# A graph propagation kernel: VectorE's running sums and first-segment sums of a batch in two runs instead of in pairs

## The chip, the core and the metric

The kernel runs on one core of a Trainium2 chip. The metric is the device time of one execution in microseconds (us). The core has a matrix engine (TensorE, PE in the rows), VectorE (DVE), ScalarE (ACT), GpSimd (POOL) and SyncE (SP), which run side by side and meet at semaphores. In this kernel SyncE starts the plain loads and stores, and GpSimd starts the indirect ones, the gathers, which fetch one table row for each of 128 partitions by an index in SBUF.

## What is computed

Four graph layers on 50000 nodes of 96 channels and 50000 edges sorted by destination, each added to its input behind a layer norm and a relu. The change touches the third, a personalised-PageRank propagation:

```python
def _L2_gnn_ref(x, edge_index):
    K = 16
    ALPHA = 0.1
    ...
    norm = (deg_inv_sqrt[row] * deg_inv_sqrt[col])[:, None]
    h = x
    for _ in range(K):
        h_neighbors = jax.ops.segment_sum(norm * h[row], col, num_segments=N)
        h = (1.0 - ALPHA) * h_neighbors + ALPHA * x
    return h
```

So 16 times over, each edge fetches the row of its source, and the rows of one destination are summed.

## The kernel before

The edges lie in order of destination, 392 per partition (`CH`), and are worked in `NB` = 49 batches of `J` = 8 columns, so a batch is 8 gathers of 128 rows of 96 floats. The sums over a destination's edges are made as a scan along each partition: `S[j] = S[j-1] * keep[j] + g[j]`, where `keep` is 0 where a new destination begins. Beside it runs `F = F + g[j] * first[j]`, the sum of the edges that belong to the first destination of the partition. It is needed only when the round is over, where a product with the matrix `B` carries sums across partitions.

The first round (`r1`) has a program of its own. The other 15 (`ROUNDS` - 1) are one hardware loop, `rounds`, with all five engines in one block, and `skewed` lets each engine take its steps on batch b with a fixed lag:

- GpSimd: `gathers`, 8 indirect DMAs from the table `y_t` of the round before into `g_` (names `r_g` in rows, line L340). There are `GB` = 4 buffers. Before a batch it waits for its indices (`s_ix`) and for VectorE to have ended batch b - 4 (`s_ss`).
- VectorE: `scan_step` (L349 running sums into `S`, rows `r_S`; L351 first-segment sums into `F`), 16 SCALAR_TENSOR_TENSOR of 128x96 floats with three inputs each, two tensors and one column of scalars. `own.settle()` behind each pair waits until both have ended. The last op of the batch increments `s_ss` ("r_sums").
- TensorE: `add` (L1421) adds `S` to the PSUM banks `pu` by products with the identity, as soon as `s_ss` has counted the batch; `start` (L1415, L1416) has put the other terms there for the next batch.
- ScalarE: `value` (L1443) scales the eight columns out of PSUM into `H`; `slots` (L1435, L1437) copies indices and scan factors for a later batch.
- SyncE: `store` (L1381) writes the batch's `H` into the other `y_t`, then `load` (L1376) fetches the constant term of a later batch.

A round begins on GpSimd only when all stores of the round before have landed (`s_st`) and so has the row of first values (`s_zo`, stored at L1386), since it gathers from that table. Between the rounds VectorE runs `finish_round` (L1248 to L1251), which waits for the product `r_pc` (L1427) and reads `F`.

Semaphores keep the name that they first got in this program. In the rows of the instruction order below `n0_ones` is VectorE's own count (`s_v`), `info_vector` is `s_ss`, `e0_ea_in_0` is the new `s_ff`, `gathered2_2` counts landed gathers, `n0_vector_stats` is `s_ix` and `n0_vector_scale` is `s_up`.

Of the kernel before, what the change touches and what calls it, by code (L numbers as in the profile page):

```python
# [19 lines left out]
D = 96  # L20
# [4 lines left out]
J = 8  # L25
NB = CH // J
# [4 lines left out]
GB = K  # L31
# [17 lines left out]
ALU = mybir.AluOpType  # L49
# [108 lines left out]
def program(nc, x, src, dst, edge_attr_32, edge_attr_96, edge_weight,  # L158
# [26 lines left out]
    with outer:  # L185
# [158 lines left out]
        def scan_step(dve, own, h, w, g, S, slots=2, s_s=None, done=None):  # L344


            for j in range(J):
                before = S[:, (h - 1) % slots, J - 1, 0:w] if j == 0 else S[:, h % slots, j - 1, 0:w]
                own.add(V.scalar_tensor_tensor(out=S[:, h % slots, j, 0:w], in0=before, scalar=scan_s[:, h, j, 0:1],  # L349
                                               in1=g[:, j, 0:w], op0=ALU.mult, op1=ALU.add))  # L350
                last = V.scalar_tensor_tensor(out=F[:, 0:w], in0=g[:, j, 0:w], scalar=scan_s[:, h, j, 1:2],  # L351
                                              in1=F[:, 0:w], op0=ALU.mult, op1=ALU.add)
                if j < J - 1 or s_s is None:
                    own.add(last)
                else:
                    last.then_inc(s_s, 1)
                own.settle()
            if s_s is not None:
                dve.wait_ge(s_s, done)

        def pointers(own, ptr, no, start, t, to, base):

# [867 lines left out]
        with ExitStack() as p5:  # L1230
# [29 lines left out]
            with nc.Block() as block:  # L1260
# [52 lines left out]
                def _(dve):  # L1313
# [16 lines left out]
                    def step(n, h):  # L1330
# [24 lines left out]
            s_v, s_ix, s_g, s_up, s_s, s_st, s_ss = (sem("r_vector"), sem("r_rows_set"), s_stream[2],  # L1355
                                                     sem("r_summed"), sem("r_values"), sem("r_stored"), sem("r_sums"))
            s_c = sems("r_start_loaded")
            s_cr, s_z, s_zo = sem("r_carry"), sem("r_first_values"), sem("r_first_stored")

            def rounds(eng, one):  # L1360
# [6 lines left out]
            with nc.Block() as block:  # L1367
# [23 lines left out]
                @block.gpsimd  # L1391
                def _(pool):
                    def one(r, odd):

                        after(pool, s_st, 16 * NB * r)
                        after(pool, s_zo, 16 * r)
                        pool.sem_inc(s_turn_p)

                        def step(b, n, h):
                            after(pool, s_ix, 2 * (r * NB + b) + 2)  # L1400
                            after(pool, s_ss, r * NB + b + 1 - GB)
                            gathers(y_t[odd], lambda j: g_[:, h % GB, j, :], h, s_g[h])
                        skewed(pool, (0, step))
                    rounds(pool, one)
# [25 lines left out]
                @block.scalar  # L1430
                def _(act):
                    def one(r, odd):
                        def slots(b, n, h):
                            s_g.wait(act, h, 16 * J * (r * OF[h] + n))
                            A.copy(idx_s[:, h, :], cols(yptr_e, b)).then_inc(s_ix, 1)  # L1435
                            after(act, s_ss, r * NB + b - 3)
                            A.copy(scan_s[:, h], cols(scan, b)).then_inc(s_ix, 1)  # L1437

                        def value(b, n, h):
                            after(act, s_up, r * NB + b + 1)  # L1440
                            v, k = cols(H, b), cols(k_e, b)
                            for j in range(J):
                                last = A.activation(v[:, j, :], pu[h % 2][j // 4][:, j % 4, :], ACT.Copy,  # L1443
                                                    scale=k[:, j:j + 1])
                            last.then_inc(s_s, 1)
                        after(act, s_ss, r * NB)
                        skewed(act, (-2, slots), (1, value))
                    rounds(act, one)

                @block.vector  # L1450
                def _(dve):
                    own = Own(dve, s_v)
                    per_batch = 2 * J - 1
                    per_round = NB * per_batch + 3

                    def one(r, odd):
                        def step(b, n, h):
                            own.base, own.n = r * per_round + b * per_batch, 0
                            after(dve, s_ix, 2 * (r * NB + b) + 2)
                            after(dve, s_up, r * NB + b - 1)  # L1460
                            s_g.wait(dve, h, 16 * J * (r * OF[h] + n + 1))
                            scan_step(dve, own, h, D, g_[:, h % GB], S, 2, s_ss, r * NB + b + 1)
                            assert own.n == per_batch
                            dve.sem_inc(s_turn_v)
                        skewed(dve, (0, step))
                        own.base, own.n = r * per_round + NB * per_batch, 0
                        finish_round(dve, own, s_cr, r + 1, zs, s_z)
                        assert own.n == 3
                        dve.wait_ge(s_z, r + 1)
                        dve.sem_inc(s_turn_v)  # L1470
                    rounds(dve, one)
# [272 lines left out]
```

## Time and profile before

| | us |
|---|---|
| median of 3 runs | 15979.43 |
| lowest and highest | 15961.53, 15987.55 |
| span of the profiled execution | 13552.9 |
| lying outside the span, against the median | 2426.5 |

The profiled execution has no device time of its own on the page; the span runs from its first to its last instruction. The propagation loop is the stretch from 4275 to 11926 us of it, 7.65 ms. In the rows a line of the timeline has the start in us, the duration in us, then engine, line, operation and tiles, and in brackets how long the engine sat idle before it and what released it. "issue" is time in which the engine waited for nothing that the profile shows. Several instructions can stand merged in one row (x2, x8).

### The profile page before, as it was taken

Reading aid. Unit: us, or ns where it says so; the run is one execution under the profiler, and the core shown is the slowest. Engines: PE = TensorE matmul, PEld = TensorE weight load, DVE = VectorE, ACT = ScalarE, POOL = GpSimd, SP = SyncE. Lnnn points to the kernel's source line nnn. Section 1 sums busy time; section 2 is a strip of 40 time slices with the busy share of each in tenths; the row PEclk is TensorE's granted clock in tenths of the full one; section 3 lists DMA queues with packets and bytes.
Section 4 is the critical chain, followed back from the end, with each engine's and each line's share of the span. In section 5 each row is a group of like instructions: output and inputs, shape, how many; then the busy total and the mean of one; then the engine's idle time right before and its main releaser. Section 6 shows DMA issues by size and latency. Waiting matters only on the chain. (4 is left out here: it accounts for less than half of the span.)

```text
span 13552.9 us, 124135 instructions
## 1 busy us (share of the span) xinstructions
PE 6161.5 (45%) x16702; PEld 3564.8 (26%) x16702; DVE 6176.6 (46%) x21955; ACT 3099.7 (23%) x11470; POOL 9980.6 (74%) x10210
## 2 busy tenths in 40 slices
PE   6422105873002555555555555555555555544000
PEld 4322103542001322223323332323322322233000
DVE  4344455596343444444444444444444444444533
ACT  5300133394000222222222222222222222233000
POOL 7677777676777777777777777777777777777777
PEclk8655557886555777777777777777777777755555
DMA  5433353374223333333333333333333333344245
GB/s 150 120 99 100 109 145 97 92 216 142 76 75 89 117 112 112 118 112 112 116 112 112 118 112 112 116 112 112 117 112 112 116 113 112 116 132 129 73 116 140
DMA packets 855833, 1558.86 MB, mean 115 GB/s; under 512 B 321698, under 2 KB 378674, under 8 KB 855666
## 3 DMA queue, kind: packets, MB, share of 16 engines
q1 hardware_dynamic: 523217, 1053.28, 22.9%
q0 software_dynamic: 332448, 504.04, 16.3%
q14 instruction: 148, 1.20, 0.0%
q8 instruction: 20, 0.33, 0.0%
HBM read 954.90 MB, written 602.08 MB: 115 GB/s over the span
## 5 line engine op out<-in xcount | busy, mean ns | idle before, releaser
L340 POOL DMA_INDIRECT r_g<-y_t,idx_s x6272 | 6051.0, 965 | 2128.7 <-issue 2115.0
L349 DVE SCALAR_TENSOR_TENSOR r_S<-r_S,scan_s,r_g 128x96 f32<-128x96 f32 x6272 | 2020.3, 322 | 4670.1 <-DMA r_g<-y_t,idx_s 3968.8
L1421 PE MATMUL r_pu<-r_S,ident 128*128 128x384 f32 x2940 | 1883.7, 787 | 3127.9 <-DVE F L351 3127.9
L1443 ACT ACTIVATE H<-r_pu,k_e 128x96 f32 (+1 forms) x5880 | 1443.3, 356 | 6059.3 <-PE r_pu L1421 6059.3
L351 DVE SCALAR_TENSOR_TENSOR F<-r_g,scan_s,F 128x96 f32<-128x96 f32 x6272 | 1967.6, 314 | 0.0
L1421 PEld LDWEIGHTS r_pu<-r_S,ident 128*128 128x128 f32 x2940 | 737.9, 276 | 3947.0 <-DVE F L351 3583.5
L1415 PE MATMUL r_pu<-H,ident 128*128 (+1 forms) x2940 | 1633.0, 646 | 101.5 <-DMA r_c<-c_t 101.5
L340 POOL DMA_INDIRECT n_ag<-agg_t,idx_s x1176 | 1227.2, 1044 | 395.8 <-issue 368.4
L1416 PE MATMUL r_pu<-r_c,ident 128*128 128x384 f32 x2940 | 1441.4, 578 | 0.0
L1415 PEld LDWEIGHTS r_pu<-H,ident 128*128 128x128 f32 x2940 | 824.4, 281 | 816.9 <-issue 683.4
L1416 PEld LDWEIGHTS r_pu<-r_c,ident 128*128 128x128 f32 x2940 | 712.4, 242 | 599.2 <-issue 383.0
L340 POOL DMA_INDIRECT e_g<-z_t,idx_s x392 | 397.2, 1013 | 148.5 <-issue 120.8
L340 POOL DMA_INDIRECT n_y<-y_t,idx_s x392 | 403.0, 1028 | 135.4 <-issue 118.0
L751 PE MATMUL e_eo<-w_e,e_eaT 97*128 97x96 f32 x784 | 182.7, 428 | 676.3 <-ACT e_eaT L772 676.3
L1297 PE MATMUL r_pc<-r_S,B 128*128 128x96 f32 x2 | 0.7, 475 | 1059.9 <-DVE H L1342 1059.9
L556 POOL DMA_INDIRECT info_t<-seg_s,idx_s x392 | 382.1, 975 | 120.2 <-issue 119.2
L1289 POOL DMA_INDIRECT r_c<-y_t,r_dst_s x392 | 378.0, 964 | 119.5 <-issue 119.5
L340 POOL DMA_INDIRECT e_kv<-kv_t,idx_s x392 | 377.9, 964 | 119.4 <-issue 119.4
L340 POOL DMA_INDIRECT e_x<-rec_t,idx_s x392 | 375.4, 958 | 119.4 <-issue 117.0
L731 POOL DMA_INDIRECT e_q<-q_t,dst_s x392 | 371.2, 947 | 119.5 <-issue 114.3
L349 DVE SCALAR_TENSOR_TENSOR e_S<-e_S,scan_s,e_g 128x96 f32<-128x96 f32 (+1 forms) x1176 | 380.3, 323 | 58.0 <-DVE e_g L800 9.4
L351 DVE SCALAR_TENSOR_TENSOR F<-e_g,scan_s,F 128x96 f32<-128x96 f32 (+1 forms) x1176 | 375.6, 319 | 0.0
(233 smaller groups left out, 7251.4 us busy)
## 6 DMA issues: line engine op xcount, KB each, us to landing
y_t<-H SPq DMA_DIRECT2D x784, 384.0 KB, 2.4
r_c<-c_t SPq DMA_DIRECT2D x735, 384.0 KB
r_g<-y_t,idx_s POOLq DMA_INDIRECT x6272
n_x<-x_t SPq DMA_DIRECT2D x147, 384.0 KB, 4.5
kv_t<-n_kvq SPq DMA_DIRECT2D x49, 768.0 KB, 3.7
agg_t<-e_S SPq DMA_DIRECT2D x98, 384.0 KB, 2.6
x_t<-n_x SPq DMA_DIRECT2D x98, 384.0 KB, 2.4
y_t<-n_y SPq DMA_DIRECT2D x98, 384.0 KB
```

Source lines behind the costliest of these rows:

```text
L340: G.indirect_dma_start(out=to(j), out_offset=None, in_=table, in_offset=bass.IndirectOffsetOnAxis(ap=idx_s[:, h, j:j + 1], axis=0)).then_i ...
L349: own.add(V.scalar_tensor_tensor(out=S[:, h % slots, j, 0:w], in0=before, scalar=scan_s[:, h, j, 0:1], in1=g[:, j, 0:w], op0=ALU.mult, op1 ...
L351: last = V.scalar_tensor_tensor(out=F[:, 0:w], in0=g[:, j, 0:w], scalar=scan_s[:, h, j, 1:2], in1=F[:, 0:w], op0=ALU.mult, op1=ALU.add)
L556: G.indirect_dma_start(out=info_t, out_offset=bass.IndirectOffsetOnAxis(ap=idx_s[:, h, j:j + 1], axis=0), in_=seg_s[:, h, j, :], in_offset ...
L731: G.indirect_dma_start(out=gq[:, h, j, :], out_offset=None, in_=q_t, in_offset=bass.IndirectOffsetOnAxis(ap=dst_s[:, h, j:j + 1], axis=0)) ...
L751: last = T.matmul(eo[g][:, j, :], eaT[:, h, g, j * P:(j + 1) * P], w_e[:], start=True, stop=True)
L1289: G.indirect_dma_start(out=cs[:, h, j, :], out_offset=None, in_=y_t[0][0:ROWS, :], in_offset=bass.IndirectOffsetOnAxis(ap=dst_s[:, h, j:j ...
L1297: T.matmul(pc[:], B[:], S[:, 0, J - 1, :], start=True, stop=True).then_inc(s_cr, 1)
L1415: T.matmul(pu[h % 2][g][:], ident[:], cols(H, b)[:, c, :], start=True, stop=False)
L1416: T.matmul(pu[h % 2][g][:], ident[:], cs[:, h % 2, c, :], start=False, stop=False)
L1421: last = T.matmul(pu[h % 2][g][:], ident[:], S[:, h % 2, 4 * g:4 * g + 4, :], start=False, stop=True)
L1443: last = A.activation(v[:, j, :], pu[h % 2][j // 4][:, j % 4, :], ACT.Copy, scale=k[:, j:j + 1])
```

## The change

In the 15 rounds of the loop VectorE no longer alternates. It does the batch's eight running sums first, each waiting for the one before, then its eight first-segment sums, each waiting for the one before. The eighth running sum increments `s_ss`, the eighth first-segment sum a new semaphore `s_ff`. TensorE still waits for `s_ss`. GpSimd and ScalarE, which need the whole batch to be done before they overwrite `g_` or `scan_s`, wait for `s_ff` instead. `r1` and the other three layers keep `scan_step`.

```diff
+        def running_sums(own, h, g, S, s_s):
+            for j in range(J):
+                before = S[:, (h - 1) % 2, J - 1, 0:D] if j == 0 else S[:, h % 2, j - 1, 0:D]
+                last = V.scalar_tensor_tensor(out=S[:, h % 2, j, 0:D], in0=before, scalar=scan_s[:, h, j, 0:1],
+                                              in1=g[:, j, 0:D], op0=ALU.mult, op1=ALU.add)
+                if j < J - 1:
+                    own.do(last)
+            last.then_inc(s_s, 1)
+
+        def first_sums(own, h, g, s_f):
+            for j in range(J):
+                last = V.scalar_tensor_tensor(out=F[:, 0:D], in0=g[:, j, 0:D], scalar=scan_s[:, h, j, 1:2],
+                                              in1=F[:, 0:D], op0=ALU.mult, op1=ALU.add)
+                if j < J - 1:
+                    own.do(last)
+            last.then_inc(s_f, 1)
...
+            s_ff = sem("r_first_sums")
...
-                            after(pool, s_ss, r * NB + b + 1 - GB)
+                            after(pool, s_ff, r * NB + b + 1 - GB)
...
-                            after(act, s_ss, r * NB + b - 3)
+                            after(act, s_ff, r * NB + b - 3)
...
-                        after(act, s_ss, r * NB)
+                        after(act, s_ff, r * NB)
...
-                    per_batch = 2 * J - 1
+                    per_batch = 2 * J - 2
...
-                            scan_step(dve, own, h, D, g_[:, h % GB], S, 2, s_ss, r * NB + b + 1)
+                            running_sums(own, h, g_[:, h % GB], S, s_ss)
+                            first_sums(own, h, g_[:, h % GB], s_ff)
+                            after(dve, s_ss, r * NB + b + 1)
+                            dve.sem_inc(s_turn_v)
+                            after(dve, s_ff, r * NB + b + 1)
```

VectorE before, in the loop of the rounds, where one batch ends and the next begins:

```order
L349 SCALAR_TENSOR_TENSOR r_S<-r_S,scan_s,r_g 128x96 [waits n0_ones]
L351 SCALAR_TENSOR_TENSOR F<-r_g,scan_s,F 128x96
L75 REGISTER_ALU
L359 REGISTER_ALU [waits n0_ones]
L108 ISA [waits info_vector]
L349 SCALAR_TENSOR_TENSOR r_S<-r_S,scan_s,r_g 128x96 [waits gathered2_2,n0_vector_scale,n0_vector_stats]
L351 SCALAR_TENSOR_TENSOR F<-r_g,scan_s,F 128x96
L75 ISA
```

A first-segment sum stands behind each running sum without a wait, and the next running sum waits for both.

VectorE now, in the middle of a batch, where the last running sums meet the first of the first-segment sums:

```order
L365 SCALAR_TENSOR_TENSOR r_S<-r_S,scan_s,r_g 128x96 [waits n0_ones]
L75 REGISTER_ALU
L365 SCALAR_TENSOR_TENSOR r_S<-r_S,scan_s,r_g 128x96 [waits n0_ones]
L374 SCALAR_TENSOR_TENSOR F<-r_g,scan_s,F 128x96
L75 REGISTER_ALU
L374 SCALAR_TENSOR_TENSOR F<-r_g,scan_s,F 128x96 [waits n0_ones]
```

Every sum now waits for the one before it on its own engine, but for the first of the eight first-segment sums, which follows the last running sum without a wait.

VectorE now, at the end of a batch:

```order
L374 SCALAR_TENSOR_TENSOR F<-r_g,scan_s,F 128x96 [waits n0_ones]
L108 REGISTER_ALU
L108 ISA [waits info_vector,e0_ea_in_0]
L365 SCALAR_TENSOR_TENSOR r_S<-r_S,scan_s,r_g 128x96 [waits gathered2_2,n0_vector_scale,n0_vector_stats]
L75 ISA
```

The running sums stand in front of the first-segment sums that they alternated with, and the batch ends with waits for both semaphores.

## Rows read from the trace of the kernel before

**Rows 1.** The page: busy time by engine, and its costliest group.

```profile
PE 6161.5 (45%) x16702; PEld 3564.8 (26%) x16702; DVE 6176.6 (46%) x21955; ACT 3099.7 (23%) x11470; POOL 9980.6 (74%) x10210
...
L340 POOL DMA_INDIRECT r_g<-y_t,idx_s x6272 | 6051.0, 965 | 2128.7 <-issue 2115.0
```

**Rows 2.** Tile r_g on POOL, loop of the rounds: duration ns min/median/max.

```profile
L340 POOL DMA_INDIRECT r_g<-y_t,idx_s x5876: 941/947/1049, 4275.1 to 11910.6; - x196
```

**Rows 3.** The same instructions, busy us (count) in that stretch.

```profile
4275.00:11911.00 7636.00, 5640.06 (x5876) 0.78 0.38 114
```

**Rows 4.** Tile r_g, a round's first batch, when VectorE is idle.

```profile
L340 POOL DMA_INDIRECT r_g<-y_t,idx_s x8: 943/946/947, 4778.8 to 4787.5; - x8
```

**Rows 5.** Timeline of one batch in the middle of a round.

```profile
6000.54 0.94 POOL L340 DMA_INDIRECT r_g<-y_t,idx_s  x1 [0.30 <-issue]
...
6003.07 0.32 DVE L349 SCALAR_TENSOR_TENSOR r_S<-r_S,scan_s,r_g 128x96 f32<-128x96 f32 x1 [5.40 <-DMA r_g<-y_t,idx_s]
6003.30 0.31 DVE L351 SCALAR_TENSOR_TENSOR F<-r_g,scan_s,F 128x96 f32<-128x96 f32 x1
6003.65 0.32 DVE L349 SCALAR_TENSOR_TENSOR r_S<-r_S,scan_s,r_g 128x96 f32<-128x96 f32 x1
...
6004.23 0.35 DVE L349 SCALAR_TENSOR_TENSOR r_S<-r_S,scan_s,r_g 128x96 f32<-128x96 f32 x1
6004.29 0.95 POOL L340 DMA_INDIRECT r_g<-y_t,idx_s  x1 [0.30 <-issue]
...
6005.43 0.32 DVE L349 SCALAR_TENSOR_TENSOR r_S<-r_S,scan_s,r_g 128x96 f32<-128x96 f32 x1
6005.54 1.02 POOL L340 DMA_INDIRECT r_g<-y_t,idx_s  x1 [0.30 <-issue]
...
6007.43 0.31 DVE L351 SCALAR_TENSOR_TENSOR F<-r_g,scan_s,F 128x96 f32<-128x96 f32 x1
6007.79 0.50 PEld L1421 LDWEIGHTS r_pu<-r_S,ident 128*128 128x128 f32 x2 [5.01 <-DVE F L351]
...
6013.11 0.35 SPq L1381 DMA_DIRECT2D y_t<-H  x1
```

**Rows 6.** Timeline: gathers that start at other distances from a sum.

```profile
8384.49 0.31 DVE L351 SCALAR_TENSOR_TENSOR F<-r_g,scan_s,F 128x96 f32<-128x96 f32 x1
8384.67 0.96 POOL L340 DMA_INDIRECT r_g<-y_t,idx_s  x1 [0.30 <-issue]
...
11539.68 0.31 DVE L351 SCALAR_TENSOR_TENSOR F<-r_g,scan_s,F 128x96 f32<-128x96 f32 x1
11539.82 1.00 POOL L340 DMA_INDIRECT r_g<-y_t,idx_s  x1 [0.30 <-issue]
```

**Rows 7.** Timeline of the end of a round and the start of the next.

```profile
5783.03 0.95 POOL L340 DMA_INDIRECT r_g<-y_t,idx_s  x1 [0.30 <-issue]
...
5785.41 0.32 DVE L349 SCALAR_TENSOR_TENSOR r_S<-r_S,scan_s,r_g 128x96 f32<-128x96 f32 x1 [5.26 <-DMA r_g<-y_t,idx_s]
...
5789.73 0.31 DVE L351 SCALAR_TENSOR_TENSOR F<-r_g,scan_s,F 128x96 f32<-128x96 f32 x1
5790.10 0.50 PEld L1421 LDWEIGHTS r_pu<-r_S,ident 128*128 128x128 f32 x2 [3.60 <-DVE F L351]
...
5793.06 1.96 ACT L1443 ACTIVATE H<-r_pu,k_e 128x96 f32<-128x96 f32 x8 [7.93 <-PE r_pu L1421]
5793.43 0.26 DVE L1248 TENSOR_TENSOR Z<-F,r_pc 128x96 f32<-128x96 f32 x1 [3.39 <-PE r_pc L1427]
...
5795.58 0.36 SPq L1386 DMA_DIRECT2D y_t<-r_zs  x1
...
5799.47 0.94 POOL L340 DMA_INDIRECT r_g<-y_t,idx_s  x1 [15.50 <-issue]
```

**Rows 8.** Timeline of the last stage: a load on SyncE's queue.

```profile
13396.24 0.38 SPq L1671 DMA_DIRECT2D n_z<-z_t  x1
```

**Rows 9.** Chain that ended last, same place: start us, us, what.

```profile
13399.38 3.31 DMA n_ag<-agg_t,idx_s
```

## The prediction, made before the changed kernel ran

> **What bounds the kernel now.** I read the page first, then the tile of the gathers, then the timeline of one batch and of one change of rounds. The page has GpSimd busy for 74% of the span, and its costliest group is the 6272 gathers `r_g`, 0.965 us each, with only "issue" between them [rows 1]. In the timeline a gather starts every 1.25 us (6004.29, 6005.54): 0.946 of its own and 0.305 of issue. VectorE sits idle 5.40 us before a batch, waiting for data [rows 5]. A batch is 8 gathers, 10.0 us. VectorE's sums take 4.67 us of that (6003.07 to the end of the last, one op behind 6007.43), so in the middle of a round VectorE, TensorE and ScalarE are all covered. Two things are not: what makes a gather longer than 0.946, and the stretch between rounds, in which GpSimd waits 15.50 us [rows 7].
>
> **Longer gathers.** The 5876 gathers of the loop are busy 5640.06 us [rows 3]; at 0.946, the median of a batch with VectorE idle, whose longest is 0.947 [rows 4], they would take 5558.7. The surplus is 81.4 us, 0.111 us per batch (735 batches); single gathers reach 1.049 [rows 2]. The timeline says when. A gather that starts 0.11 us after the start of a sum takes 1.02 [rows 5], 0.14 after 1.00, 0.18 after 0.96 [rows 6]. One that starts 0.06 after takes 0.95, and there it is the sum that is longer, 0.35 for 0.32 [rows 5]. So a gather loses (0.19 - p) when it starts p behind a sum's start, for p from about 0.09 (a choice between the 0.06 and the 0.11 of the rows) to 0.19, and nothing otherwise. GpSimd sets the pace, so each loss is paid in full.
>
> The Trainium skill (SBUF — State Buffer, "Who interferes with whom") says that VectorE with two SBUF inputs and GpSimd reading SBUF share a port under an exclusive lock, and that the first to start keeps it for its whole instruction, the other blocking fully. The rows agree that one of the two waits and that order decides, but a gather is let in 0.19 into a sum of 0.32. Were it held to the sum's end, the triangle of Part 3 would be 0.23 by 0.23, 0.026, and an even spread would give 0.33 per batch before and after alike: no gain from Part 3, where the rows give 37 us.
>
> **Part 1: the order on VectorE.** A pair now takes 0.58 (6003.07 to 6003.65), since the second sum starts 0.23 into the first. Under the change a sum waits for the one before: 0.32 plus the gap between an end and a dependent start (6003.61 to 6003.65, some 0.035), 0.354 a step; only the ninth starts 0.23 after the eighth. The running sums end 7 x 0.354 + 0.32 = 2.80 after the start, all sixteen after some 5.50, against 4.67. VectorE's extra 0.83 us (610 us over 735 batches) costs nothing in a round: it has 5.40 idle. If that cover were gone it would all be paid. The register operations and the second wait at the batch's end go the same way. GpSimd's and ScalarE's waits for `s_ff` look four batches back, some 30 us, and are met long before.
>
> **Part 2: the end of a round.** Here the chain is bare: last gather ends 5783.98, its rows are there and the first sum starts 5785.41, last sum ends 5790.04, products 5790.10, ScalarE 5793.06 for 1.96, the stores, and GpSimd again at 5799.47 [rows 7]. TensorE starts 4.69 after the first sum now, and 2.80 + 0.06 = 2.86 with the change: 1.83 earlier. `finish_round` must not become late instead: it starts 3.39 after the last sum, on the carry product; the product moves up with the rest and comes 2.86 + 3.33 = 6.2 after the first sum, the first-segment sums end at 5.5. So the whole tail moves up 1.83, 15 times (each round of the loop, the last into the next stage): 27 us at most.
>
> Some is given back. SyncE's store of a batch now falls together with the next batch's first sum (6013.11, 10.04 after 6003.07, and a batch is 10.1) [rows 5]. It moves to 1.8 before that, which is when the batch's last gather is in flight. In a round that gather's rows are there 1.43 to 1.59 after its end (5785.41 - 5783.98, 6003.07 - 6001.48) [rows 5, 7]. What a gather does with a 384 KB transfer beside it shows in the last stage: a load goes out at 13396.24, and of the gathers around it the last takes 3.31 to land [rows 8, 9]. So landing may cost 0 to 1.8 more. I take 1.3 in half the rounds, because a batch that is 1.3 late sends its own store 1.3 later, out of the way of the next: late and punctual batches should alternate. That is 0.65 off 1.83 on average, with a further 0.2 for rounds with TensorE's clock high, where the store comes sooner still: 1.0 x 15 = **15 us** gained, bounds 0 and 27.
>
> **Part 3: gathers against sums.** Per sum the loss, averaged over where a gather may start, is a triangle of 0.10 by 0.10, 0.005 us^2. Spread evenly, the pairs would cost a gather 2 x 0.005 / 0.58 = 0.017, and 3.7 gathers start in 4.67 us: 0.064 per batch. Measured is 0.111, so they are bunched: the first sum starts together with a gather (both wait on the pace of GpSimd), the next gather comes 1.25 later, 0.08 behind the third pair's start (1.17), and the one after that 0.11 behind a running sum, as the 6005.54 one does. The new spacing breaks this. With 0.354, gathers at -0.03 + 1.25k: the first falls 0.16 behind a sum's start (loss 0.03), the second 0.02 (none), the third 0.34 (none), the fourth 0.17 (0.02): 0.05. In a batch that is 1.3 late they fall at 1.17 (0.11 behind, loss 0.08), 2.4 and later without loss or nearly: 0.08. Spread evenly: 0.005 / 0.354 x 4.4 gathers in 5.5 us = 0.062. I take 0.06. The gain is (0.111 - 0.060) x 735 = **37 us**. The bounds: 0.02 if the sum that waits pushes its followers along and keeps them clear of the next gather (gain 67), and 0.26 if three gathers each lose 0.085 (loss 110).
>
> **Sum.** 15 + 37 = 52 us, made against the span of 13552.9, which becomes 13501. What lies outside the span (2426.5 against the median) is taken as unchanged: 15979 - 52 = **15927**. What a measurement of this kernel can tell from no change is about 0.2%, 32 us.
>
> **Rivals.** (a) The bunching stays as bad, in other places: Part 3 gives 0 to 15, the tail 15, so 15955 to 15965. For it: 0.111 is itself above an even spread, so bunching is a habit of this loop, where the first sum is locked to a gather. Against: the steps above land outside the window. The same time comes out if the surplus has nothing to do with the sums; against that stands 0.947 as the longest with VectorE idle [rows 4]. The Trainium skill, same page and section, infers that `tensor_tensor` on VectorE does not hold up the making of descriptors; by it the gather term would be nil and only the tail be left, and the rows at 0.11, 0.14 and 0.18 speak against it. (b) Slower: seven steps are 2.48 and two gathers 2.50, so gathers come back to nearly the same place behind a sum every second time. If that place is 0.09 to 0.13, three gathers of a batch lose 0.085 each, 0.255 per batch: (0.255 - 0.111) x 735 = 106 lost, less 15: 16070. It turns to a loss of over 32 us from 0.175 per batch on. It hangs on 0.05 us in the moment of the first sum against the gather beside it, which the rows put at 0.03 behind; that is the reason for a real chance. (c) The tail gains nothing, because the last gather always lands late, while Part 3 holds: 15942. (d) Nothing moves up, because TensorE waits for something else than `s_ss`: in the timeline it starts 0.05 after the last sum in every batch shown, so hardly any chance.
>
> **Chances.** Forecast, a gain of 35 to 85: 0.62 (with (c) in it). (a) 0.27. (b) and what lies between it and no change 0.09, most of it a loss over 32. (d) 0.02. The forecast's own range is 15895 to 15945. For 8 in 10 I leave out the far end of (b) and the largest gains: 15890 to 15985. Faster by over 0.2%: 0.65; within: 0.28; slower: 0.07.
>
> **What would show it.** Right: the tile `r_g` in the loop busy some 37 us less at the same count; gathers over 1.0 about half as many per batch, now also late in the sums; the product L1421 some 2.87 after the batch's first sum; first sums that alternate between 1.5 and 2.9 after the last gather's end; GpSimd's wait between rounds 13.7 where the last batch is punctual and about 15 where it is not, 14.5 in the mean. Wrong: a gather mean of 0.960 or more, or VectorE waited for by GpSimd in the middle of a round, or `finish_round` waiting on its own last sum.

## The result, and the profile after

The change made the kernel slower: 16151.7 us (median of 4 runs, 16143 to 16173) against 15983.5 (median of 4 runs beside them, 15962 to 16003), a ratio of 1.0106 [1.0092, 1.0121]. The prediction, 15927 in a range of 15890 to 15985, was wrong in sign.

The page of the profiled run of the changed kernel, first lines and two groups (line, engine, operation, count | busy us, mean ns | idle us before, main releaser):

```profile
span 16152.7 us, 129251 instructions
...
PE 6115.5 (38%) x16702; PEld 3532.6 (22%) x16702; DVE 6612.8 (41%) x21955; ACT 3091.5 (19%) x11470; POOL 9821.3 (61%) x10210
...
L340 POOL DMA_INDIRECT r_g<-y_t,idx_s x6272 | 5979.8, 953 | 3867.3 <-issue 2193.0
...
L374 DVE SCALAR_TENSOR_TENSOR F<-r_g,scan_s,F 128x96 f32<-128x96 f32 x5880 | 1872.7, 318 | 1253.4 <-issue 1037.7
```

Against [rows 1] the gathers did get shorter, 953 ns for 965. But the idle time before them went from 2128.7 to 3867.3 us, and GpSimd is busy for 61% of the span where it was for 74%. VectorE now has 1253.4 us of idle time in front of its first-segment sums, 1037.7 of it with nothing to wait for. The span itself is 2600 us longer than that of the profiled run of before, 13552.9, while the times differ by 168. So the two profiles can't be compared as they stand: the execution that I had read was of another kind than those that were timed. I had seen the 2426.5 us between its span and the median, and had carried them over as a constant.

The waits of the changed kernel in the middle of the rounds, 5100 to 11200 us (engine, tile, line <- releaser: us in total, times, longest):

```profile
PE r_pu L1435 <- DMA r_c<-c_t: 2156.4, 280, 20.5
...
POOL r_g L340 <- ACT scan_s L1457: 1060.7, 143, 9.5
...
DVE r_S L365 <- issue: 957.4, 564, 11.7
...
DVE F L374 <- issue: 695.6, 691, 1.9
```

And one stretch of its timeline (start us, us, engine, line, operation [idle before <- releaser]):

```profile
6423.77 0.73 SPq L1401 DMA_DIRECT2D y_t<-H  x1
...
6426.67 0.32 DVE L365 SCALAR_TENSOR_TENSOR r_S<-r_S,scan_s,r_g 128x96 f32<-128x96 f32 x1 [1.09 <-issue]
...
6428.07 0.39 DVE L365 SCALAR_TENSOR_TENSOR r_S<-r_S,scan_s,r_g 128x96 f32<-128x96 f32 x1 [1.08 <-issue]
...
6429.41 0.94 POOL L340 DMA_INDIRECT r_g<-y_t,idx_s  x1 [0.30 <-issue]
...
6430.81 0.70 SPq L1396 DMA_DIRECT2D r_c<-c_t  x1
...
6484.60 1.96 ACT L1463 ACTIVATE H<-r_pu,k_e 128x96 f32 x8 [20.50 <-remote]
...
6487.64 1.03 POOL L340 DMA_INDIRECT r_g<-y_t,idx_s  x1 [7.36 <-ACT scan_s L1457]
```

Here two sums are 1.40 us apart, where Part 1 had reckoned 0.354. Between them stands one register instruction (one that reads or sets an engine's own counters), here with the wait for the sum before. The views don't print these; the trace's own records do, and this one lasts 0.70 us, where it is 0.04 to 0.1 elsewhere. SyncE's issue of a transfer takes 0.73 and 0.70 in place of 0.35. GpSimd goes on at its 1.25 us all the while. I call this **slow issue**: by their records, SyncE, VectorE and ScalarE issue slowly or not at all, in stretches of 8 to 25 us that come about every 36 us. In the trace that I had predicted from, no register or semaphore instruction of these engines takes 0.6 to 0.8 us. In the profiled run of after 1935 of SyncE's do, 3028 of VectorE's and 185 of ScalarE's.

The records have limits in such a stretch. VectorE's sums fit the engine that waits for them: TensorE's product follows the recorded end of a batch's last running sum by 0.05 us or more in all 735 batches. SyncE's times don't. A store recorded as issued at 6467.43 has its 144 packets moved from 6465.40 to 6466.61, before that. And the traces with slow issue hold 92 to 102 thousand records of semaphore events, the others 445 to 456 thousand, so that "remote" (no recorded instruction raised the semaphore) and the other releasers are less sure there.

### The profile page after: what moved, and what is told of

It is laid out like the page before. It is cut to its first block and busy times, and to the rows that moved or that the text cites. A ratio compares the mean times of both kernels' runs of the same rounds, so it can differ in the third digit from the quotient of the medians.

```text
span 16152.7 us, 129251 instructions
## 1 busy us (share of the span) xinstructions
PE 6115.5 (38%) x16702; PEld 3532.6 (22%) x16702; DVE 6612.8 (41%) x21955; ACT 3091.5 (19%) x11470; POOL 9821.3 (61%) x10210
## 5 line engine op out<-in xcount | busy, mean ns | idle before, releaser
L340 POOL DMA_INDIRECT r_g<-y_t,idx_s x6272 | 5979.8, 953 | 3867.3 <-issue 2193.0
L365 DVE SCALAR_TENSOR_TENSOR r_S<-r_S,scan_s,r_g 128x96 f32<-128x96 f32 x5880 | 1882.7, 320 | 4233.0 <-remote 1762.3
L1435 PE MATMUL r_pu<-H,ident 128*128 (+1 forms) x2940 | 1817.6, 712 | 3557.5 <-DMA r_c<-c_t 3284.8
L374 DVE SCALAR_TENSOR_TENSOR F<-r_g,scan_s,F 128x96 f32<-128x96 f32 x5880 | 1872.7, 318 | 1253.4 <-issue 1037.7
L1441 PE MATMUL r_pu<-r_S,ident 128*128 128x384 f32 x2940 | 1322.8, 580 | 1472.7 <-DVE r_S L365 969.7
L1435 PEld LDWEIGHTS r_pu<-H,ident 128*128 128x128 f32 x2940 | 740.3, 271 | 4327.4 <-issue 3853.9
L1436 PE MATMUL r_pu<-r_c,ident 128*128 128x384 f32 x2940 | 1626.4, 645 | 0.0
L1441 PEld LDWEIGHTS r_pu<-r_S,ident 128*128 128x128 f32 x2940 | 655.8, 231 | 2066.6 <-DVE r_S L365 1058.4
L1436 PEld LDWEIGHTS r_pu<-r_c,ident 128*128 128x128 f32 x2940 | 786.6, 268 | 665.7 <-issue 496.5
L647 PE MATMUL n_ob<-w_kvq,n_hT 97*128 97x288 f32 x784 | 305.3, 535 | 318.3 <-issue 196.7
```

The source lines that it names most:

```text
L340: G.indirect_dma_start(out=to(j), out_offset=None, in_=table, in_offset=bass.IndirectOffsetOnAxis(ap=idx_s[:, h, j:j + 1], axis=0)).then_i ...
L365: last = V.scalar_tensor_tensor(out=S[:, h % 2, j, 0:D], in0=before, scalar=scan_s[:, h, j, 0:1], in1=g[:, j, 0:D], op0=ALU.mult, op1=ALU.add)
L374: last = V.scalar_tensor_tensor(out=F[:, 0:D], in0=g[:, j, 0:D], scalar=scan_s[:, h, j, 1:2], in1=F[:, 0:D], op0=ALU.mult, op1=ALU.add)
L647: T.matmul(ob[j % 4][:], hT[:, h, j // 4, j % 4 * P:(j % 4 + 1) * P], w_kvq[:], start=True, stop=True).then_inc(s_om, 1)
L1435: T.matmul(pu[h % 2][g][:], ident[:], cols(H, b)[:, c, :], start=True, stop=False)
L1436: T.matmul(pu[h % 2][g][:], ident[:], cs[:, h % 2, c, :], start=False, stop=False)
```

## The experiments

Three theories. **I (instructions):** the loss is the change's register instructions. It gives VectorE 7 more per batch, a wait behind nearly every sum and the second wait and turn at the end (129251 instructions against 124135, 5116 more), and under slow issue each is dear. **O (order):** the loss is the new order and spacing of the sums. **N (neither):** the change has nothing to do with it, and the two kernels met different conditions. The expectations name two more: **W**, a finer form of the first, in which the waits between dependent sums are dear and not their number of instructions, and **R**, in which register and semaphore instructions alone are dear. A job is one visit to a chip, with the kernel before run beside the others, and shows only what its own condition shows: the kernel before took 15.89 to 16.01 ms in some jobs (slow issue) and 13.47 to 13.53 ms in the others (none). I could not choose. Without slow issue most kernels ran several times, which gave an interval; with it, the runs of my own are single ones, whose difference from the kernel before of the same job I give.

**The same two kernels again.** No edit.

> The kernel before, unchanged, for a second profile. The trace of before read so far spans 13552.9 us while its timed runs took 15961 to 16003; the trace of the changed kernel spans 16152.7 and its timed runs 16143 to 16173. In that trace 3028 register and semaphore instructions of VectorE and 1935 of SyncE take 0.6 to 0.8 us each (0.04 normally), where the first trace of before has none. Theory A (slow instruction issue is in every run of both kernels, and the first trace of before is the exception): span about 15980, with some 2000 to 3000 such instructions on VectorE. Theory B (it comes with the change): span about 13550 and no such instructions, though the timed run says 15980.

> The changed kernel, unchanged, on the same chip. Both theories: span about 16150, with about 3000 slow instructions on VectorE and 2000 on SyncE. If it spans about 13500, the slow issue is a state that a profile falls into or not, whatever the kernel.

Measured: 15899.5 for the kernel before and 16042.4 for the change, with 15891.5 for the kernel before of that job: +151. With N there should have been none. The page of the kernel before with slow issue, its span and the gathers' group:

```profile
span 15897.7 us, 124135 instructions
...
L340 POOL DMA_INDIRECT r_g<-y_t,idx_s x6272 | 6020.3, 960 | 3597.2 <-issue 2334.3
```

Its waits, 5100 to 11200 us:

```profile
PE r_pu L1415 <- DMA r_c<-c_t: 2647.7, 315, 19.4
...
POOL r_g L340 <- ACT scan_s L1437: 829.4, 123, 10.3
```

Its timeline, where one such stretch reaches GpSimd:

```profile
6463.35 1.45 PE L1421 MATMUL r_pu<-r_S,ident 128*128 128x384 f32 x4
...
6470.69 0.69 SPq L1376 DMA_DIRECT2D r_c<-c_t  x1
...
6471.44 1.64 PE L1415 MATMUL r_pu<-H,ident 128*128 x2 [6.63 <-DMA r_c<-c_t]
...
6482.75 0.32 DVE L349 SCALAR_TENSOR_TENSOR r_S<-r_S,scan_s,r_g 128x96 f32<-128x96 f32 x1 [15.68 <-remote]
6482.76 1.96 ACT L1443 ACTIVATE H<-r_pu,k_e 128x96 f32 x8 [19.51 <-remote]
...
6485.80 1.00 POOL L340 DMA_INDIRECT r_g<-y_t,idx_s  x1 [4.90 <-ACT scan_s L1437]
```

So slow issue is there before the change too. Two things are late. SyncE sends a batch's load late and TensorE waits for it (6.63 us). And ScalarE's values come late by more than that: the product that they wait for ended at 6464.80, yet they start at 6482.76, and VectorE, which waits for the same product, starts 0.01 from them. Without slow issue, in before and in a2 below, the values start 0.04 to 0.25 us after their product's end; here they start over 5 us after it in 393 of 735 batches, in the profile of the change above in 371. Behind the values come the copies `idx_s` and `scan_s`, and GpSimd, which has nothing but issue before its gathers in [rows 5], waits for those. In the first trace of before the same window has 80.7 us of waiting for `r_c` and none for `scan_s`. What differs by kernel is VectorE: 0 of its register instructions take 0.6 to 0.8 us in this run of before, 2456 in that of the change. GpSimd's wait for `scan_s` goes from 829.4 to 1001.7 us there, and to 1060.7 in the profile above.

These two runs come from one job, so their traces tell where the loss lies. Between the first and the last memset of `finish_round` the 15 rounds take 9028.2 us before and 9173.3 with the change, 145 more; the rest of the span differs by 2. In the rounds the gathers themselves are 27 us shorter, as forecast. GpSimd's idle time is 13 us longer between the rounds and 160 inside them.

**The order and the instructions apart.** Two kernels keep the order of the kernel before. One waits for every sum of a pair, which gives the change's 7 further register instructions per batch and nearly its spacing; the other leaves the sums alone and adds 7 increments of a semaphore, for which nobody waits. Each ran in both conditions. The first, c1 and c1s, against the kernel before:

```diff
-scan_step(dve, own, h, D, g_[:, h % GB], S, 2, s_ss, r * NB + b + 1)
+for j in range(J):
+    before = ...
+    own.do(V.scalar_tensor_tensor(out=S[:, h % 2, j, 0:D], ...))
+    last = V.scalar_tensor_tensor(out=F[:, 0:D], ...)
+    if j < J - 1:
+        own.do(last)
+last.then_inc(s_ss, 1)
+dve.wait_ge(s_ss, r * NB + b + 1)
```

The second, c2 and c2s:

```diff
 scan_step(dve, own, h, D, g_[:, h % GB], S, 2, s_ss, r * NB + b + 1)
+for _ in range(7):
+    dve.sem_inc(s_turn_v)
```

> The kernel before with its alternating order, but each of the sixteen sums of a batch waits for the one before, as in the change: 7 more register instructions on VectorE per batch, and 5.5 us of sums for 4.67. Theory I (issue): the rounds lose time in stretches where VectorE, ScalarE and SyncE issue an instruction per 0.7 us or nothing, and every instruction more on VectorE makes that dearer; then about 150 us slower than before (the change: 16042 against 15892 on this chip), with 1500 or more VectorE register instructions of 0.6 to 0.8 us. Theory O (order): what costs is that the first-segment sums come last, late for GpSimd and ScalarE; then within 30 us of before.

> The kernel before, with 7 semaphore increments that nobody waits for behind each batch on VectorE (5145 in all), no other change; 5116 instructions are what the change adds. Theory I: 100 to 200 us slower than before. Theory W (it is not the number of instructions but the waits between sums, 0.83 us more of sums per batch): within 30 us of before.

> The same kernel as c1_pairs_settled (order as before, each sum waits for the one before), for the same purpose. With slow issue, theory I and theory W both: 1.006 to 1.012; theory O (the order): 0.997 to 1.003. Without slow issue it repeats 0.9974.

> The same kernel as c2_dummies_dve (7 unused semaphore increments per batch on VectorE, order as before), sent again in the hope of the condition with slow issue, which is the one in which the change was measured. There, theory I (each instruction more on VectorE is dear): 100 to 200 us slower than before, ratio 1.006 to 1.012. Theory W (it is the waits between dependent sums, each of which is exposed to a slow register instruction): ratio 0.998 to 1.002. Without slow issue it repeats 1.000.

Measured without slow issue: c1 0.9974 [0.9963, 0.9985], c2 1.0003 [0.9992, 1.0014]. With it: c1s 16208.8 and c2s 16207.1 against 16009.6, +199 and +197. Seven unused increments per batch, which cost nothing in one condition, cost more than the whole change in the other, with the order of the sums untouched. That is theory I, and it speaks against W. The order is not needed for the loss: c1s, with as many instructions as the change and the old order, loses 199, the change 151 and 168. These are single runs against a single run of before; the 199 and 197 are far over the 41 us between the four runs of before beside the change. The expectations of c1 and c2, 150 and 100 to 200 us slower, were not borne out in the jobs without slow issue and were in the one with it. The waits of c2s in the same window:

```profile
DVE r_S L349 <- issue: 826.9, 391, 17.0
...
POOL r_g L340 <- ACT scan_s L1437: 1013.2, 142, 10.8
```

And those of c1s:

```profile
DVE r_S L1464 <- issue: 1011.3, 717, 9.4
...
DVE F L1466 <- issue: 743.0, 709, 1.8
...
POOL r_g L340 <- ACT scan_s L1437: 1054.8, 137, 11.0
```

**Fewer sums; the same increments on another engine.** c3 leaves the first-segment sums of the rounds out, so what they compute is missing from its result; with 7 waits a batch it has one register instruction less on VectorE than the kernel before. c4 is the kernel before with the 7 unused increments on TensorE. The edit of c3 and c3s:

```diff
-per_batch = 2 * J - 1
+per_batch = J - 1
...
-scan_step(dve, own, h, D, g_[:, h % GB], S, 2, s_ss, r * NB + b + 1)
+for j in range(J):
+    before = ...
+    last = V.scalar_tensor_tensor(out=S[:, h % 2, j, 0:D], ...)
+    if j < J - 1:
+        own.do(last)
+last.then_inc(s_ss, 1)
+dve.wait_ge(s_ss, r * NB + b + 1)
```

And of c4 and c4s, in TensorE's batch:

```diff
 last.then_inc(s_up, 1)
+for _ in range(7):
+    pe.sem_inc(s_turn_pe)
```

> The eight first-segment sums of each batch are left out (the result lacks them); running sums alone, each waiting for the one before. VectorE issues 8 instructions fewer per batch and its sums take 2.8 us. Theory I: 100 to 200 us faster than before, though VectorE sat idle more than 4 us per batch already. Theory O and W: what is left is a shorter tail of the rounds and fewer held-up gathers, 15 x 1.8 and 735 x 0.05 us: 30 to 65 us faster.

> The kernel before, with 7 semaphore increments that nobody waits for behind each batch's add on TensorE, which shows no slow issue in any trace so far. If the cost of an instruction is one of the whole core, 100 to 200 us slower as with VectorE; if it belongs to the engine that issues it, within 30 us of before.

> The same kernel as c3_no_first (the first-segment sums of the rounds are left out, running sums each wait), sent again for the condition with slow issue, since c2s and c1s have just shown 1.0123 and 1.0124 there. Theory I: VectorE has 8 sums per batch fewer and as many register instructions less one, so the time falls by more than the 70 us of the other condition: 150 to 250 us faster than before. Theory W, with waits as the exposed thing, which are 7 for 8 here: 30 to 80 us faster. Without slow issue it repeats 0.995.

> The same kernel as c4_dummies_pe (7 unused increments per batch on TensorE), for the same purpose. With slow issue: 150 to 250 us slower if an instruction is dear on whichever engine, as 7 on VectorE cost 197 us; within 40 us if it is dear only on the engines that show slow register instructions (VectorE, SyncE, ScalarE).

Without slow issue: c3 0.9950 [0.9927, 0.9972], c4 0.9999 [0.9988, 1.0010]. With it: c3s 15866.8 and c4s 16000.7 against 15926.0, so -59 and +75. With VectorE's instructions not increased, the running sums alone keep their gain (-70 and -59). Theory I had asked for 150 to 250 us there and W for 30 to 80, so this one missed for I: eight sums fewer per batch, with nearly as many register instructions, give back no more under slow issue than without. It is further register instructions that are shown to be dear, and not that any instruction less is a gain. On TensorE the increments cost less than half of what they cost on VectorE, between the two forecasts of c4s (150 to 250, and within 40), though as single runs both c3s and c4s are uncertain by some tens of us: the kernel before itself was at 15891, 15926 and 16010 in three jobs. TensorE itself has 4 register instructions of 0.6 to 0.8 us in c4s, so there the loss is not made on the engine that has the increments; how it arises stays open.

**The change without slow issue.**

> The changed kernel again, since the kernel before took 15892 us in one job and 13471 in the next: there are two conditions, one with the slow issue (before near 15900 to 15980) and one without (near 13470). If this job is without, the prediction's own steps are tested: 52 us faster than before, ratio 0.996, tile r_g busy some 37 us less in the loop. Each settled pair alone gave 0.9974 there. If it is with slow issue: ratio 1.009 to 1.011 as in the two comparisons so far.

Measured: 13446.1 against 13526.6, 0.9938 [0.9922, 0.9955], 81 us faster, where 52 and 0.996 were expected. The page of this run:

```profile
span 13442.9 us, 129251 instructions
...
L340 POOL DMA_INDIRECT r_g<-y_t,idx_s x6272 | 5990.1, 955 | 2093.9 <-issue 2081.8
...
L374 DVE SCALAR_TENSOR_TENSOR F<-r_g,scan_s,F 128x96 f32<-128x96 f32 x5880 | 1870.1, 318 | 181.8
```

VectorE's idle time before the first-segment sums is 181.8 us here and 1253.4 above, for the same code. The next fence is the end of a round, to be laid beside [rows 7]:

```profile
5752.52 0.35 SPq L1401 DMA_DIRECT2D y_t<-H  x1
...
5753.54 0.94 POOL L340 DMA_INDIRECT r_g<-y_t,idx_s  x1 [0.30 <-issue]
...
5757.31 2.80 DVE L365 SCALAR_TENSOR_TENSOR r_S<-r_S,scan_s,r_g 128x96 f32<-128x96 f32 x8 [5.79 <-DMA r_g<-y_t,idx_s]
...
5763.59 0.94 POOL L340 DMA_INDIRECT r_g<-y_t,idx_s  x1 [0.30 <-issue]
...
5766.08 2.90 DVE L365 SCALAR_TENSOR_TENSOR r_S<-r_S,scan_s,r_g 128x96 f32<-128x96 f32 x8 [3.27 <-DMA r_g<-y_t,idx_s]
5768.90 2.79 DVE L374 SCALAR_TENSOR_TENSOR F<-r_g,scan_s,F 128x96 f32<-128x96 f32 x8
5769.03 1.56 PE L1441 MATMUL r_pu<-r_S,ident 128*128 128x384 f32 x4 [1.69 <-DVE r_S L365]
...
5770.63 1.96 ACT L1463 ACTIVATE H<-r_pu,k_e 128x96 f32<-128x96 f32 x8 [5.54 <-PE r_pu L1441]
5771.91 0.25 DVE L1267 TENSOR_TENSOR Z<-F,r_pc 128x96 f32<-128x96 f32 x1 [0.23 <-DVE F L374]
...
5777.29 0.94 POOL L340 DMA_INDIRECT r_g<-y_t,idx_s  x1 [12.76 <-issue]
```

The last batch's first sum comes 1.55 us after its last gather's end, and TensorE 2.95 after that (4.69 before). ScalarE follows after 1.60, where it was 2.96, because TensorE here meets the higher of its two clock levels: the granted clock is 1.00 over these four products, 0.39 each, and was 0.50 over the four of [rows 7], 0.73 each. GpSimd waits 12.76 for 15.50. In the batch before that one a store was issued 1.02 ahead of the last gather, and the first sum came 2.83 after that gather's end (5753.54 + 0.94 to 5757.31). `finish_round` now waits for its own last sum, 0.23.

To split the 81 us I compare the 15 rounds between the first and the last memset of `finish_round`, in this run and in c2 (tile F, line: count, durations in ns, first start to last start), c2 being the kernel before with increments that cost nothing here:

```profile
L1268 DVE MEMSET F<- x16: 145/145/145, 4260.3 to 11819.3; 128x104 f32 x16
```

The same row of c2:

```profile
L1249 DVE MEMSET F<- x16: 145/145/145, 4250.9 to 11869.8; 128x104 f32 x16
```

7559.0 against 7618.9; c4 has 7622.0, the first trace of before 7656.8. Of the 61 us against c2 and c4, 27 are gathers (5880 of 0.9496 us, against 0.9540 and 0.9543), and 33 are the 14 waits between these rounds (12.40 us in the mean, against 14.68 and 14.76). This doesn't split the 81. c2 and c4 come from a job in which the kernel before took 13470.7, not 13526.6, and outside the rounds, where the code is the same, a2 is 29 us longer than c2. No trace of before was kept from a2's own job. Two jobs below have kernels with and without the new order side by side (e3 is the change less one wait, e1 the kernel before with memsets that cost nothing): there the rounds are 59 us shorter, 26 of it gathers and 31 waits between rounds, and 45 us shorter, 13 and 30. c1 loses at the ends of rounds (15.89) and wins more in the gathers (0.9471): with a wait behind each sum, and so a spacing of 0.354 from first to last, they suffer least of all. c3, which has no second sums, has 0.9467.

**What could be taken off the change.** d1 lets the first-segment sums alternate between two accumulators (11 waits per batch, not 14, though an expectation says 15; 3000 instructions over the kernel before, not 5100). e3 drops the first of the two waits at the batch's end and its turn, which is one instruction per batch (128516 in its trace, against 129251), so six over the kernel before and not five, as an expectation below has it. e1 is the kernel before with 7 small memsets per batch on VectorE, to tell whether any further instruction is dear under slow issue, or register instructions only. The edits of d1 and e3 against the change, and of e1 against the kernel before:

```diff
+F2 = sb("F2", [P, D])
...
-for j in range(J):
+for j in range(0, J, 2):
...
+    last = V.scalar_tensor_tensor(out=F2[:], in0=g[:, j + 1, 0:D], ...)
...
+    own.settle()
```

```diff
-after(dve, s_ss, r * NB + b + 1)
-dve.sem_inc(s_turn_v)
```

```diff
+for j in range(7):
+    V.memset(spare[:, j, :], 0.0)
```

> The changed kernel with its first-segment sums in two accumulators, F and F2, that alternate: they run as pairs again (one added at the end of a round), so VectorE waits 11 times per batch instead of 15 and its sums take 5.1 us for 5.5, while the running sums still come first. In the condition without slow issue (before near 13470 to 13530): the tail's gain is kept, the gathers meet pairs again for half of the time: ratio 0.994 to 0.997, not better than the change's 0.9938. In the condition with slow issue (before near 15900): if VectorE's register instructions are what costs, 4 fewer than the change per batch: 1.004 to 1.006 where the change has 1.0095 to 1.0106; if the order is what costs, 1.009 to 1.011.

> The change without the wait for the running sums' signal at a batch's end and without one of its two turn increments: one semaphore instruction fewer per batch on VectorE. With slow issue, theory R: 20 to 40 us better than the change, ratio to before 1.007 to 1.009; theory I the same. Without slow issue: 0.994, as the change.

> The kernel before with 7 memsets of 128x16 into a spare tile behind each batch on VectorE, which nobody reads or waits for. Theory R (in the condition with slow issue only register and semaphore instructions of VectorE are dear): within 60 us of before. Theory I (every instruction of VectorE): 150 to 250 us slower, as 7 increments cost 197. Without slow issue both: within 30 us of before.

> The same kernel as d1_two_chains (running sums first, first-segment sums in two interleaved chains), whose VectorE has about 3 register instructions per batch more than before where the change has 7. With slow issue, theory R: 40 to 90 us slower than before, ratio 1.0025 to 1.006; theory I the same less the order's gain. Without slow issue it repeats 0.996.

> The kernel before with seven memsets of 128x16 per batch on VectorE, whose output nobody reads. Should the job have the slow issue (15.9 ms for the kernel before), this tells which instructions are dear there. If only register and semaphore instructions are: within 30 us of the kernel before of the same job. If any further VectorE instruction is: +100 to +200 us, as the seven unused register increments per batch gave (+197). Without the slow issue: no difference, as in its first run (1.0001).

> The change without the wait on s_ss at the batch's end and without one of its two turn increments: five instead of seven more register instructions per batch than the kernel before. With the slow issue, if the loss goes with their number: +90 to +120 us against the kernel before, where the change has +151 to +168. If it is the order of the sums that loses there: as the change, +150 or more. Without the slow issue: -50 to -80.

> The change with the first-segment sums on two accumulators that alternate: eleven waits on VectorE's own semaphore per batch instead of fourteen, so some four register instructions more than the kernel before. With the slow issue, if the loss goes with their number: +60 to +100 us; if it is the order of the sums: +150 or more. Without the slow issue: about -55, as twice before (0.9959 and 0.9957).

None of these seven runs met slow issue (the kernel before took 13471 to 13501 in their jobs), so they don't answer what they were made for. They gave d1 0.9959 [0.9941, 0.9977], d1s 0.9957 [0.9944, 0.9971] and d1t 13431.9 against 13477.2; e3 0.9959 [0.9940, 0.9979] and e3t 13431.7 against 13477.2; e1 1.0001 [0.9990, 1.0012] and e1t 13475.8 against 13477.2. Without slow issue neither the second turn nor the three waits nor seven memsets are worth anything that can be measured. A gain is there each time in which the running sums come first, at 45 to 58 us, less than the 81 of a2.

**What stays open.** That further instructions on VectorE suffice for such a loss is shown by c2s and c1s, one run each; the change with fewer of them never met slow issue. Each of these kernels also has a longer program, and no run adds length without adding executed instructions. Which kinds count is not shown either: the records of the stretch above have the transfer issues of SyncE on the same pace of 0.70 us as the register instructions, and a sum every 1.40 with one wait between, which looks like a pace per instruction of any kind; no run tested it. Nor is it known why VectorE's register instructions are nearly spared as long as it has no more of them than the kernel before (of 14784 none slow in b1 and one in c4s, 108 of 14054 in c3s) and are hit so hard with a third more (2456 to 3234 of some 19900 in four runs), and whether d1, with fewer, would lose less.

What slow issue comes from is not known. More loading of instructions is not seen: the DMA queue that the page calls "instruction" has 148 packets in the first trace of before and 148 in b1. A rival that no run tests is the recording itself. The traces with slow issue lack four fifths of the semaphore records, and SyncE's records in them fall behind its transfers; an instruction more would then cost because it leaves a record more. All timed runs but the first of before list their core's span and granted clock, which come from such records, so nothing here shows whether either kernel would meet slow issue unrecorded.

## Why the prediction was wrong

**The step that failed** is the last sentence but one of Part 1: "The register operations and the second wait at the batch's end go the same way", that is, they cost nothing since VectorE has 5.40 us idle. The rows of before could not price them, and I hid them behind the cover of an undisturbed trace without asking for its worth in the executions that were timed. Seven such instructions more per batch, without the new order, cost 197 us there (c2s), and the change lost 151 to 168. Together with them failed the sentence under **Sum**, that what lies outside the span "is taken as unchanged". Those 2426.5 us were no fixed piece outside the span; they were the difference between two conditions, and in the timed one VectorE has no such cover: its instructions take 0.7 us each in stretches, and 16 sums with 14 waits between them, which Part 1 has at 5.5 us, take about 17 (6422.46 to 6439.73). Inside the rounds GpSimd then sits idle 160 us more (a1 against b1). Through which of the waits the one leads to the other was not traced.

**Part 1, the spacing:** right. Eight running sums take 2.80, TensorE starts 2.85 to 2.97 after the first (the last batches of the 15 rounds of a2).

**Part 2, the end of a round:** right in its mechanism, the size too small. Reckoned at 1.0 us a round with a bound of 1.83; measured 2.3 in a2, 33 to 35 us in all for 15, and 30 or 31 for 14 in the two jobs with e1 and e3. It lies outside the bound of 27. Two terms were off. The alternation between punctual and late batches came as forecast: over 14 rounds 45% of the batches of a2 have their first sum over 2.2 us after the last gather, 0.6% in before. But a round has 49 batches and begins with a punctual one, so the last is punctual every time: 1.44 to 1.60 in all 14, and nothing is given back. And I held the products at the length they had, and took 0.2 off for rounds with a high clock, a term for which no row stood. The runs show the opposite sign: TensorE found the clock high in 12 of 15 rounds of a2 (about 1.6 us from its start to ScalarE's; 1.88 in the mean, 2.65 in before and 2.49 in c2), 0.6 to 0.8 more. In e3 the mean is 2.23 against 2.70 in e1, so that share differs by run. One sign that was to show the forecast wrong did come, `finish_round` waiting for its own last sum. It waited 0.23 us, and the tail was shorter all the same.

**Part 3, gathers against sums:** right in its mechanism, and near in size in part by luck. Forecast 37 us, measured 27 against c2 and c4, 26 and 13 in the jobs with e1 and e3, 61 against the trace that the forecast was made from (5644.4 us of gathers, 5583.4 now). The rule of (0.19 - p) holds: in a2 the gathers that start 0.11 to 0.13 us behind a sum's start take 1.016 in the mean, those at 0.15 to 0.17 take 0.971, and those at 0.19 to 0.22 take 0.944, as with no sum beside them. Gathers over 1.0 us were to be half as many; they are 128 in a2, 760 in c2 and 1041 in the first trace. What is left of the loss sits in many small ones (1022 over 0.955), as a spacing without a habit gives. The first trace had more bunching than two later ones of nearly the same kernel, so the 0.111 per batch that I built on was itself high: 0.064 in c2 (5609.8 less 5880 x 0.946, over 735). The 0.060 for the new order was high as well, 0.028 in a2, and the two errors offset each other in the difference, 0.051 forecast and 0.036 against c2.

**The sum:** 52 forecast. Without slow issue 45 to 59 in the rounds where both orders ran in one job, and in the whole 45 to 58 there and 81 in a2's job, [61, 105]. With slow issue the change lost 151 to 168. That is about 199 for seven instructions per batch less 31 to 48 for the order, if the difference between the change and c1s, measured in different jobs, is put down to the order; no run shows that.

**The rivals:** none was it. (b), the slower one, had gathers bunching against sums, and the runs show the contrary. A rival "the executions that are timed differ in kind from the one profiled, and instructions are dear there" was what was missing. The clue stood in the table ahead of the prediction: a profiled time 15% under the median.

## What to carry to other kernels

Compare the profiled run's own time with the timed ones before anything else; where they are far apart, the trace shows another regime, and no cost that it shows as hidden may be carried over. Register and semaphore instructions beside the critical path cost nothing here in one condition and some 200 us in the other, so between two forms that do the same, take the one with fewer. Where an instruction's record and the transfer that it starts disagree, trust the transfer. A change that is a gain by its order and a loss by its instructions is best split into kernels with one of each; seven unused increments settled here what no reading did.

## What the runs showed that I had not expected

- The same kernel takes 13.47 or 15.9 to 16.0 ms from one job to another, with no change of code. In the slower condition the records of SyncE, VectorE and ScalarE fall to 0.7 us an instruction in stretches, and GpSimd's don't. ScalarE's values start up to 26 us after the product that they wait for, where it is 0.25 at most otherwise.
- Seven unused increments per batch on VectorE (5145 in all) cost 197 us in one condition, 1.0003 [0.9992, 1.0014] in the other.
- The first sum on a gather's rows starts 1.5 us after its end when no store has been issued in the 6 us before that (a2, median 1.54, longest 1.70), and 2.6 to 3.2 (medians) when one of 384 KB was issued 0.5 to 2 us before it; the longest is 3.95. Over all batches the median is 1.68 and the 95th percentile 3.11 in a2, 1.55 and 1.66 in before.
- Waiting for each sum before the next (c1) makes the kernel faster without slow issue, 0.9974, since the gathers beside the sums are then shorter (0.9471 us for 0.9540). The Trainium skill (SBUF — State Buffer, "SBUF: two separate sides" and "Who interferes with whom") has the first of the two keep the port for its whole instruction, under an exclusive lock. The runs agree that the starts decide, but not that the other is shut out to the end: in c1, 1021 gathers start 0.19 to 0.22 us behind the start of a sum of 0.32, and take 0.943 in the mean, no more than those with no sum beside them.
